# Cross-attention of a decoder layer: one transpose per head for the maxima, a reordered opening, moved value projections and border waits

## Chip, cores and metric

The kernel runs on one core of a Trainium2 chip. The metric is the device time of one execution in microseconds (us). TensorE multiplies matrices into PSUM, VectorE, ScalarE and GpSimd work on elements, SyncE issues DMAs and waits for them. Each engine runs its own instructions in order; semaphores tie them together.

## The reference

A pre-norm decoder layer with B=4, T=512, D=512: self-attention, cross-attention over 1024 context rows, and a quantised feed-forward. The part around the change, for each batch:

```python
Q = (query @ Wq).reshape(b, q_len, G, Hpg, dh) / sqrt(dh)   # G=4 groups, Hpg=4, dh=32
K = (key @ Wk).reshape(b, kv_len, G, dh)
V = (value @ Wv).reshape(b, kv_len, G, dh)
scores = einsum('bqghd,bkgd->bghqk', Q, K) + m * (k - q)    # m: slope of the head
w = softmax(where(mask, scores, min), axis=-1)
out = einsum('bghqk,bkgd->bqghd', w, V).reshape(b, q_len, 512) @ Wo
x = x + out
```

## The kernel before

Three phases follow one another, each with its own block of five instruction streams. A block ends with a barrier over all engines; behind it GpSimd clears the phase's semaphores (line 44).

**Cross-attention** (from line 780) handles 64 heads (4 batches of 16, in groups of 4). A head has four units (c, r), and the loop over `UNITS` is the same on every engine. Scores are made twice. In the first form (line 1353, tile `ps_a`, two banks) queries are rows; VectorE takes the maximum of each row (line 1224). The maxima of a head, 128x4 for each of four query tiles, with three columns of slope values beside them, are transposed (line 1365) and copied as rows 96 to 99 of `Q` (line 1233), so that the second form (line 1341, `ps_b`, keys are rows) gives scores less their maximum. ScalarE takes the exponential (line 1082) and its rounded part (line 1109), GpSimd the remainder (line 1275), and TensorE multiplies both with the values (lines 1381, 1382, 1386). First scores run two heads ahead of the second, value products three units behind.

`ORDER` (line 864) lists twelve jobs of a batch: projections of queries, keys and values and the output products of the batch before. A job has four pieces, one a unit, and a new job begins every five units. The first two value jobs lie in the eight units ahead of the first exponential. Output products wait for the normalised group `aT` (line 1301).

**Opening** (lines 1194, 1303): keys of batch 0, statistics, normalisation, transposes, queries of groups 0 and 1; then SyncE spreads keys and queries over partitions by DMA (lines 918 to 946), three DMAs a head and five a group of keys. All of group 0 must have landed before the first scores. **End** (lines 1000 to 1014): the last four output tiles are added to x1 rows from a ring of three buffers and stored; SyncE waits for all stores. The feed-forward loads x2 rows and an identity, and GpSimd computes the reciprocal deviation (line 1729).

## Time and profile before

| | |
|---|---|
| median of 3 runs | 1785.76 us (1784.31 to 1786.4) |
| profiled execution | 1786.3 us, its span 1784.2 us |
| TensorE busy | 1650.0 us (92%) |
| ScalarE / GpSimd / VectorE busy | 1236.8 / 1175.4 / 1158.1 us |
| mean granted clock of TensorE | 0.982 |
| DMA moved | 110.76 MB |

Self-attention ends at about 667 us, cross-attention at about 1456, the feed-forward at 1781. The busy times are sums over phases with different limits; the chain of work that ended last covers only the feed-forward, so the two phases before must be read from timelines.

### The profile page before, as it was taken

Reading aid. Unit: us, or ns where it says so; the run is one execution under the profiler, and the core shown is the slowest. Engines: PE = TensorE matmul, PEld = TensorE weight load, DVE = VectorE, ACT = ScalarE, POOL = GpSimd, SP = SyncE. Lnnn points to the kernel's source line nnn. Section 1 sums busy time; section 2 is a strip of 40 time slices with the busy share of each in tenths; the row PEclk is TensorE's granted clock in tenths of the full one; section 3 lists DMA queues with packets and bytes.
Section 4 is the critical chain, followed back from the end, with each engine's and each line's share of the span. In section 5 each row is a group of like instructions: output and inputs, shape, how many; then the busy total and the mean of one; then the engine's idle time right before and its main releaser. Section 6 shows DMA issues by size and latency. Waiting matters only on the chain. (4 is left out here: it accounts for less than half of the span.)

```text
span 1784.2 us, 24902 instructions
## 1 busy us (share of the span) xinstructions
PE 1650.0 (92%) x8112; PEld 1161.7 (65%) x8112; DVE 1158.1 (65%) x2031; ACT 1236.8 (69%) x2018; POOL 1175.4 (66%) x1080
## 2 busy tenths in 40 slices
...
GB/s 225 95 60 85 95 126 113 85 103 105 101 13 13 31 12 73 130 42 13 77 77 45 27 74 70 25 36 28 63 24 34 114 113 1 25 25 37 25 19 24
DMA packets 57647, 110.76 MB, mean 62 GB/s; under 512 B 9132, under 2 KB 13996, under 8 KB 57136
## 3 DMA queue, kind: packets, MB, share of 16 engines
...
## 5 line engine op out<-in xcount | busy, mean ns | idle before, releaser
L1275 POOL TENSOR_TENSOR x_p_lo<-x_p,x_p_hi 128x1024 fp32r<-128x1024 f32 x192 | 455.5, 2384 | 258.5 <-ACT x_p_hi L1109 258.0
L1224 DVE TENSOR_REDUCE x_maxes<-x_ps_a 128x1 f32<-128x1024 f32 x256 | 312.8, 1222 | 227.6 <-PE x_ps_a L1353 226.1
L1082 ACT ACTIVATE x_p<-x_ps_b,x_any_valid 128x1024 f32<-128x1024 f32 x256 | 285.1, 1114 | 129.6 <-PE x_ps_b L1341 128.2
L1341 PE MATMUL x_ps_b<-x_Q,x_K 100*128 100x512 f32 x512 | 226.4, 523 | 5.6 <-ACT x_p L1082 4.4
L1109 ACT ACTIVATE x_p_hi<-x_p 128x1024 fp32r<-128x1024 f32 x192 | 203.2, 1058 | 4.8
L1353 PE MATMUL x_ps_a<-x_K,x_Q 99*128 99x512 f32 x512 | 164.8, 403 | 10.6 <-DMA x_Q<-x_p_lo 8.8
L1381 PE MATMUL x_ps_o<-x_p_hi,x_V 128*96 128x512 f32 x384 | 157.1, 409 | 1.2 <-POOL x_p_lo L1275 1.2
L1341 PEld LDWEIGHTS x_ps_b<-x_Q,x_K 100*128 100x128 f32 x512 | 90.2, 190 | 97.8 <-issue 74.0
L1382 PE MATMUL x_ps_o<-x_p_lo,x_V 128*96 128x512 f32 x384 | 150.9, 393 | 0.0
L435 ACT ACTIVATE a_work<-a_ps_s,a_neg_max,a_q_r 128x256 f32<-128x256 f32 (+1 forms) x256 | 133.9, 539 | 4.5 <-DVE a_neg_max L535 4.5
L627 POOL TENSOR_TENSOR a_work<-a_work,a_inv_den 128x1024 f32<-128x1024 f32 (+1 forms) x64 | 109.9, 1717 | 18.7 <-DVE a_inv_den L575 18.7
L1386 PE MATMUL x_ps_o<-x_p,x_V 128*96 128x512 f32 x256 | 120.4, 591 | 0.0
L1353 PEld LDWEIGHTS x_ps_a<-x_K,x_Q 99*128 99x128 f32 x512 | 94.0, 190 | 40.4 <-issue 10.8
L616 POOL TENSOR_TENSOR a_q_r<-a_q_ss,a_half_neg 128x4 f32<-128x4 f32 x64 | 65.1, 1017 | 76.7 <-DVE a_q_ss L553 74.9
L633 PE MATMUL a_ps_out<-a_w_hi,a_aT_hi 128*128 128x512 f32 x256 | 108.8, 425 | 1.4 <-DVE a_aT_lo L496 1.4
L634 PE MATMUL a_ps_out<-a_w_lo,a_aT_hi 128*128 128x512 f32 x256 | 102.6, 401 | 0.0
L635 PE MATMUL a_ps_out<-a_w_hi,a_aT_lo 128*128 128x512 f32 x256 | 102.5, 400 | 0.0
L420 ACT ACTIVATE a_qT_hi<-a_ps_front 128x512 fp32r<-128x512 f32 x64 | 38.2, 597 | 64.8 <-PE a_ps_front L694 64.8
L602 POOL TENSOR_TENSOR a_work<-a_q 128x512 f32<-128x512 f32 x64 | 66.5, 1038 | 18.8 <-ACT a_q L458 18.8
L496 DVE TENSOR_TENSOR a_aT_lo<-a_ps_a,a_aT_hi 128x512 fp32r<-128x512 f32 x64 | 44.3, 692 | 51.0 <-ACT a_aT_hi L379 50.5
L1382 PEld LDWEIGHTS x_ps_o<-x_p_lo,x_V 128*96 128x96 f32 x384 | 62.4, 163 | 22.4
L1381 PEld LDWEIGHTS x_ps_o<-x_p_hi,x_V 128*96 128x96 f32 x384 | 62.0, 161 | 22.9 <-POOL x_p_lo L1275 2.0
...
## 6 DMA issues: line engine op xcount, KB each, us to landing
...
```

The costliest lines, as they stand in the source:

```text
L435: act.activation(p[:, c % 2, j, 0:w], ps_s[:, j, 0:w], ACT.Exp, scale=q_r[:, c % 4, j:j + 1], bias=neg_max[:, c % 2, j:j + 1], accum_out=r ...
L627: pool.tensor_tensor(out=p[:, c % 2, :, 0:w], in0=p[:, c % 2, :, 0:w], in1=inv_den[:, c % 2, :].unsqueeze(2).to_broadcast([P, G1, w]), op= ...
L633: pe.matmul(out_ap, hi, rhs_hi, start=start, stop=False)
L1082: act.activation(p[:, r, :, :], ps_b[:, :, :], ACT.Exp, scale=any_valid[:, b % 2:b % 2 + 1]).then_inc(exp_ready, 1)
L1109: act.activation(p_hi[:, r], p[:, r], ACT.Copy).then_inc(hi_ready, 1)
L1224: dve.tensor_reduce(out=maxes[:, h2, r, 3:4], in_=ps_a[:, :, :], axis=mybir.AxisListType.XY, op=ALU.max)\
L1275: pool.tensor_tensor(out=p_lo[:, r], in0=p[:, r], in1=p_hi[:, r].bitcast(F32), op=ALU.subtract).then_inc(lo_ready, 1)
L1341: last = pe.matmul(ps_b[:, j, :], K[0:ROWS + 4, g, kb * P:(kb + 1) * P], Q[0:ROWS + 4, hh, :], start=True, stop=True)
L1353: last = pe.matmul(ps_a[:, j, :], Q[0:ROWS + 3, h2, r * P:(r + 1) * P], K[0:ROWS + 3, g2, j * 512:(j + 1) * 512], start=True, stop=True)
L1381: pe.matmul(bank[0:ROWS, :], vs, p_hi[:, rw, j], start=(rw == 0 and j == 0), stop=False)
L1382: last = pe.matmul(bank[0:ROWS, :], vs, p_lo[:, rw, j], start=False, stop=False)
L1386: last = pe.matmul(bank[0:ROWS, :], V32[:, bw % 2, j, gw, :], p[:, 3, j], start=False, stop=(j == 1))
```

## The change

- The slope columns and maxima of a head stand in one 128x128 buffer, 32 columns apart, two buffers in turn; one transpose makes four blocks of rows, copied by four casts. VectorE refills the slope columns.
- The opening: barrier without a wait for the x1 stores (SyncE waits later); statistics first, slope rows split between VectorE and GpSimd, memsets on GpSimd, key rows in two parts; head 0's rows are copied by ScalarE and VectorE and not by DMA; the first eight first scores alternate between `ps_a` and `ps_b`; the output weights load later.
- One of the first two value jobs moves into the loop; in later batches the first value job comes ahead of the output products. The jobs of batch 0 shift by five units, the norms of the next batch by a head.
- The last four x1 rows are all loaded ahead; the barrier waits for one store. The feed-forward waits for the others before its loads, and the identity is loaded once for all phases.
- Semaphores are cleared in ranges.

```diff
...
-    for s in sems:
-        nc.gpsimd.sem_clear(s)
+    nums = sorted(s.num for s in sems)
+    first = 0
+    for k in range(1, len(nums) + 1):
+        if k == len(nums) or nums[k] != nums[k - 1] + 1:
+            nc.gpsimd.sem_clear(range(nums[first], nums[k - 1] + 1))
+            first = k
...
+        ident = stack.enter_context(nc.sbuf_tensor("ident", [P, P], F32))
+        ident_bf = stack.enter_context(nc.sbuf_tensor("ident_bf", [P, P], BF16))
+        rows = stack.enter_context(nc.sbuf_tensor("rows", [P, 3, D], F32))
+        x1_stored = [stack.enter_context(nc.semaphore(f"x1_stored{j}")) for j in range(2)]
+        x2_stored = [stack.enter_context(nc.semaphore(f"x2_stored{j}")) for j in range(3)]
...
-            for j in range(2):
-                sp.wait_ge(x1_stored[j], 16 * (TILES // 2))
...
+            act.activation(ident_bf[:, :], ident[:, :], ACT.Copy).then_inc(round_ready, 1)
...
-        maxes = sb("maxes", [P, HX, TPB, 4])
+        maxes = sb("maxes", [P, 2, P])
...
-        ORDER = (("Q", 2, 0), ("Q", 3, 0), ("K", 0, 1), ("K", 1, 1), ("out", 0, -1), ("out", 1, -1), ("out", 2, -1), ("out", 3, -1),
-                 ("Q", 0, 1), ("V", 0, 1), ("V", 1, 1), ("Q", 1, 1))
+        ORDER = (("Q", 2, 0), ("Q", 3, 0), ("K", 0, 1), ("K", 1, 1), ("V", 0, 1), ("out", 0, -1), ("out", 1, -1), ("out", 2, -1),
+                 ("out", 3, -1), ("Q", 0, 1), ("V", 1, 1), ("Q", 1, 1))
...
-        for b in range(-1, B):
-            jobs = [(8 * b + 4 * (n - 9), (name, i, 0)) for n, (name, i, later) in enumerate(ORDER) if name == "V"] if b < 0 else \
-                [(4 * HX * b + 5 * n, (name, i, b + later)) for n, (name, i, later) in enumerate(ORDER) if 0 <= b + later < B]
+        def add_job(u, job):
+            for k in range(4):
+                pieces[divmod(u + k, 4)] = job, k
+            finished.append(job)
+            finished_at[divmod(u + 3, 4)] = job
+        add_job(-4, ("V", 0, 0))
+        add_job(0, ("V", 1, 0))
+        for b in range(B):
+            for n, (name, i, later) in enumerate(ORDER):
+                if 0 <= b + later < B:
+                    add_job(4 * HX * b + 5 * (n + 1 if b == 0 and n < 5 else n), (name, i, b + later))
...
-            return (hh - 2, b + 1) if r == 3 and 0 <= c < HEADS and 2 <= hh < 6 and b + 1 < B else None
+            i = hh - (2 if b else 3)
+            return (i, b + 1) if r == 3 and 0 <= c < HEADS and 0 <= i < TPB and b + 1 < B else None
...
+        def scores_bank(n):
+            return ps_b if n < 8 and n % 2 else ps_a
+        def queries_spread(g, b):
+            return 192 * (b + 1) - (48 if g == 0 else 0)
+        def last_rows(i):
+            return hT[:, 0, :] if i == 0 else x1t[:, (TPB * (B - 1) + i) % 3, :]
...
-                for j in range(HPG):
+                for j in range(1 if b == g == 0 else 0, HPG):
...
             load_mask(0)
-            sp.dma_start(wo_sb[:, :, :], wo.rearrange("(c p) n -> p c n", p=P)).then_inc(wo_in, 16)
...
             spread_keys(0, 3)
+            sp.dma_start(wo_sb[:, :, :], wo.rearrange("(c p) n -> p c n", p=P)).then_inc(wo_in, 16)
+            for j in range(2):
+                sp.wait_ge(x1_stored[j], 16 * (TILES // 2))
...
-            for i in range(3):
-                load_residual(B - 1, i)
+            for i in range(TPB):
+                k = TPB * (B - 1) + i
+                if i:
+                    sp.wait_ge(x2_stored[k % 3], 16 * 4)
+                sp.dma_start(last_rows(i), x1_rows[k * P:(k + 1) * P, :]).then_inc(res_in[k % 3] if i else last_in, 16)
...
-                sp.dma_start(x2_rows[k * P:(k + 1) * P, :], x1t[:, k % 3, :]).then_inc(x2_stored[k % 3], 16)
-                if i == 0:
-                    load_residual(B - 1, 3)
-            for j in range(3):
-                sp.wait_ge(x2_stored[j], 16 * len(range(j, TILES, 3)))
+                sp.dma_start(x2_rows[k * P:(k + 1) * P, :], last_rows(i)).then_inc(x2_stored[k % 3] if i else last_stored, 16)
+            sp.wait_ge(last_stored, 16)
...
+            def first_k(i):
+                act.wait_ge(first_k_made, i + 1)
+                act.activation(k_hi[:, i * 512:(i + 1) * 512], ps_b[:, i, :], ACT.Copy).then_inc(first_k_hi_ready, 1)
+            def key_rows_of(groups):
+                act.activation(K[ROWS:ROWS + 4, groups, :], key_rows[ROWS:ROWS + 4, :].unsqueeze(1).broadcast_to(
+                    [4, groups.stop - groups.start, S]), ACT.Copy).then_inc(k_rows_ready, 1)
+            first_k(0)
+            act.wait_ge(rows_in, 32)
+            key_rows_of(slice(0, 1))
...
-            for i in range(2):
-                act.wait_ge(first_k_made, i + 1)
-                act.activation(k_hi[:, i * 512:(i + 1) * 512], ps_b[:, i, :], ACT.Copy).then_inc(first_k_hi_ready, 1)
+            first_k(1)
...
-            act.wait_ge(const_in, 48)
-            act.activation(K[ROWS:ROWS + 4, :, :], key_rows[ROWS:ROWS + 4, :].unsqueeze(1).broadcast_to([4, GX, S]), ACT.Copy)\
-                .then_inc(k_rows_ready, 1)
...
+                if i == 0:
+                    act.activation(Q[0:DH, 0, :], bank[0:DH, :], ACT.Copy, scale=QSCALE).then_inc(head0_hi_ready, 1)
+                    act.wait_ge(head0_hi_ready, 1)
+                    act.activation(Q[DH:2 * DH, 0, :], Q[0:DH, 0, :].bitcast(F32), ACT.Copy).then_inc(head0_hi_ready, 1)
+                    act.wait_ge(head0_lo_ready, 1)
...
+            key_rows_of(slice(1, GX))
+            act.wait_ge(k_rows_ready, 2)
...
-            dve.memset(half_neg[:, :], -0.5).then_inc(ones_ready, 1)
-            dve.memset(V[:, :, :, :, 2 * DH:].bitcast(F32), 1.0).then_inc(ones_ready, 1)
-            dve.memset(V32[:, :, :, :, DH:2 * DH], 0.0).then_inc(ones_ready, 1)
-            dve.memset(V32[:, :, :, :, 2 * DH:], 1.0).then_inc(ones_ready, 1)
+            dve.memset(half_neg[:, :], -0.5).then_inc(half_ready, 1)
...
+            def slope_columns(c):
+                if c >= 2:
+                    dve.wait_ge(max_made, c - 1)
+                at = maxes[:, c % 2, :].rearrange("p (j a) -> p j a", a=32)
+                dve.tensor_copy(at[:, :, 0:3], slope_cols[:, c % HX, 0:3].unsqueeze(1).broadcast_to([P, TPB, 3])).then_inc(slope_ready, 1)
...
+            for i in range(TPB):
+                statistics(0, i)
+            variances(0)
+            first_k(0)
+            biases(0)
+            mask_to_row(0)
+            first_k(1)
+            valid(0)
+            dve.wait_ge(cols_in, 16)
+            dve.wait_ge(ones_ready, 1)
+            for c in range(2):
+                slope_columns(c)
+            dve.wait_ge(rows_in, 32)
+            dve.tensor_copy(Q[ROWS:ROWS + 4, 0:HPG, :], slopes[ROWS:ROWS + 4, 0:HPG].unsqueeze(2).broadcast_to([4, HPG, T]))\
+                .then_inc(q_rows_ready, 1)
...
+                if i == 0:
+                    dve.wait_ge(first_q_made, 1)
+                    dve.wait_ge(head0_hi_ready, 1)
+                    dve.scalar_tensor_tensor(out=Q[2 * DH:3 * DH, 0, :], in0=bank[0:DH, :], scalar=QSCALE, in1=Q[0:DH, 0, :].bitcast(F32),
+                                             op0=ALU.mult, op1=ALU.subtract).then_inc(head0_lo_ready, 1)
...
-                    if n == 0:
-                        dve.wait_ge(maxes_in, 16)
-                    if c + 2 >= HX and r == 0:
-                        dve.wait_ge(max_made, c + 2 - HX + 1)
-                    dve.tensor_reduce(out=maxes[:, h2, r, 3:4], in_=ps_a[:, :, :], axis=mybir.AxisListType.XY, op=ALU.max)\
-                        .then_inc(max_ready, 1)
+                    if c >= 0 and r == 0:
+                        dve.wait_ge(max_made, c + 1)
+                    dve.tensor_reduce(out=maxes[:, c % 2, 32 * r + 3:32 * r + 4], in_=scores_bank(n)[:, :, :], axis=mybir.AxisListType.XY,
+                                      op=ALU.max).then_inc(max_ready, 1)
...
-                    dve.tensor_copy(Q[ROWS:ROWS + 4, (c + 1) % HX, :], ps_x[0:4, :]).then_inc(max_row_ready, 1)
+                    for j in range(TPB):
+                        dve.tensor_copy(Q[ROWS:ROWS + 4, (c + 1) % HX, j * P:(j + 1) * P], ps_x[32 * j:32 * j + 4, 0:P])\
+                            .then_inc(max_row_ready, 1)
+                if r == 3 and 2 <= c + 3 < HEADS:
+                    slope_columns(c + 3)
...
+            pool.memset(maxes[:, :, :], 0.0).then_inc(ones_ready, 1)
+            pool.memset(V[:, :, :, :, 2 * DH:].bitcast(F32), 1.0).then_inc(ones_ready, 1)
+            pool.wait_ge(half_ready, 1)
...
+            pool.memset(V32[:, :, :, :, DH:2 * DH], 0.0).then_inc(ones_ready, 1)
+            pool.memset(V32[:, :, :, :, 2 * DH:], 1.0).then_inc(ones_ready, 1)
+            pool.wait_ge(rstd_ready, 1)
+            pool.wait_ge(ones_ready, 4)
+            pool.wait_ge(rows_in, 32)
+            pool.tensor_copy(Q[ROWS:ROWS + 4, HPG:, :], slopes[ROWS:ROWS + 4, HPG:].unsqueeze(2).broadcast_to([4, HX - HPG, T]))\
+                .then_inc(q_rows_ready, 1)
+            pool.wait_ge(q_rows_ready, 2)
...
-            pe.wait_ge(wo_in, 16)
-            pe.wait_ge(q_rows_ready, 1)
-            pe.wait_ge(ones_ready, 4)
+            pe.wait_ge(q_rows_ready, 2)
+            pe.wait_ge(head0_hi_ready, 2)
+            pe.wait_ge(head0_lo_ready, 1)
...
                     if r == 0:
-                        pe.wait_ge(max_row_ready, c + 1)
+                        pe.wait_ge(max_row_ready, TPB * (c + 1))
...
-                        pe.wait_ge(first_k_lo_ready, 2)
+                        pe.wait_ge(max_ready, 8)
...
                     if r == 0 and h2 % HPG == 0:
-                        pe.wait_ge(q_spread[g2], 192 * (b2 + 1))
+                        if n:
+                            pe.wait_ge(q_spread[g2], queries_spread(g2, b2))
...
-                    if n:
-                        pe.wait_ge(max_ready, n)
+                    if n == 0:
+                        pe.wait_ge(first_k_lo_ready, 2)
+                    if n == 4:
+                        pe.wait_ge(q_spread[0], queries_spread(0, 0))
+                    if n >= 2:
+                        pe.wait_ge(max_ready, n if n > 8 else n - 1)
...
                     for j in range(2):
-                        last = pe.matmul(ps_a[:, j, :], Q[0:ROWS + 3, h2, r * P:(r + 1) * P], K[0:ROWS + 3, g2, j * 512:(j + 1) * 512],
+                        last = pe.matmul(scores_bank(n)[:, j, :], Q[0:ROWS + 3, h2, r * P:(r + 1) * P], K[0:ROWS + 3, g2, j * 512:(j + 1) * 512],
...
+                    pe.wait_ge(slope_ready, c + 2)
...
-                        pe.wait_ge(max_row_ready, c + 1)
+                        pe.wait_ge(max_row_ready, TPB * (c + 1))
...
-                    for j in range(TPB):
-                        last = pe.transpose(ps_x[0:4, j * P:(j + 1) * P], maxes[:, (c + 1) % HX, j, :], ident[:, :])
-                    last.then_inc(max_made, 1)
+                    pe.transpose(ps_x[:, 0:P], maxes[:, (c + 1) % 2, :], ident[:, :]).then_inc(max_made, 1)
...
-                    if rw == 0 and kw % HX == 0:
-                        pe.wait_ge(job_read, jobs_until("V", 1, bw))
+                    if w == 0:
+                        pe.wait_ge(ones_ready, 4)
+                    if rw in (0, 2) and kw % HX == 0:
...
+            for j in range(3):
+                sp.wait_ge(x2_stored[j], 16 * 5)
...
-                if c == -3:
-                    dve.wait_ge(ident_in, 16)
-                    dve.tensor_copy(ident_bf[:, :], ident[:, :]).then_inc(const_ready, 1)
...
```

## Rows read from the trace of the kernel before

**Rows 1.** Busy time by engine in one stretch: stretch, length, PE, PEld, DVE, ACT, POOL, clock.
```profile
725.26:1437.87 712.61, 701.25 (x2784) 441.61 (x2783) 480.33 (x522) 580.46 (x629) 477.58 (x210) 1.00 0.18 53
```

**Rows 2.** Timeline of VectorE, border: start, length, instruction [idle before, releaser].
```profile
665.86 0.69 DVE L523 TENSOR_TENSOR a_work<-a_ps_out,a_xt 128x512 f32<-128x512 f32 x1 [3.16 <-PE a_ps_out L635]
...
669.13 0.06 DVE L1113 MEMSET x_half_neg<- 128x4 f32 x1 [2.59 <-PEq L113]
```

**Rows 3.** Timeline of TensorE, opening of cross-attention.
```profile
669.25 8.80 PE L1307 MATMUL x_ps_b<-shared 128*128 128x512 f32 x16 [3.43 <-PEq L113]
...
691.25 3.67 PE L1321 MATMUL x_ps_j<-x_hT,shared 128*128 128x512 f32 x8 [1.37 <-ACT x_hT L1061]
...
694.76 3.60 PE L1321 MATMUL x_ps_x<-x_hT,shared 128*128 128x512 f32 x8
...
707.21 1.19 PE L1353 MATMUL x_ps_a<-x_K,x_Q 99*128 99x512 f32 x2 [8.85 <-DMA x_Q<-x_p_lo]
...
714.76 1.05 PE L1291 MATMUL x_ps_j<-shared 128*128 128x128 f32 x8
...
725.26 0.70 PE L1341 MATMUL x_ps_b<-x_Q,x_K 100*128 100x512 f32 x2
```

**Rows 4.** Timelines of VectorE and ScalarE, opening of cross-attention.
```profile
675.88 4.42 DVE L1195 CAST x_Q<-x_slopes 4x8192 fp32r<-4x8192 f32 x1 [3.98 <-DMA x_p<-in_c_key_rows]
...
685.03 0.58 DVE L1132 TENSOR_SCALAR x_ln_bias<-x_mv,x_ln_rstd 128x1 f32<-128x1 f32 x4 [1.19 <-POOL x_ln_rstd L1258]
...
710.87 1.23 DVE L1224 TENSOR_REDUCE x_maxes<-x_ps_a 128x1 f32<-128x1024 f32 x1 [1.21 <-PE x_ps_a L1353]
...
727.84 0.41 DVE L1164 TENSOR_TENSOR x_V<-x_ps_j,x_V 128x256 fp32r<-128x256 f32 x1
...
685.28 2.93 ACT L1026 ACTIVATE shared<-shared,x_ln_bias,x_ln_rstd 128x512 f32<-128x512 f32 x4 [23.31 <-DVE x_ln_bias L1132]
```

**Rows 5.** Timeline of SyncE's DMA issues: first and twelfth of group 0's queries.
```profile
697.98 0.59 SPq L944 DMA_DIRECT2D x_Q<-x_p_hi  x1
...
704.94 0.59 SPq L946 DMA_DIRECT2D x_Q<-x_p_lo  x1
```

**Rows 6.** Timeline of TensorE in the middle of the stage, around one head's transposes.
```profile
1007.65 0.60 PE L1365 MATMUL x_ps_x<-x_ident,x_maxes 128*4 128x128 f32 x4
1008.00 0.48 PE L1381 MATMUL x_ps_o<-x_p_hi,x_V 128*96 128x512 f32 x1
1008.32 0.39 PE L1382 MATMUL x_ps_o<-x_p_lo,x_V 128*96 128x512 f32 x1
```

**Rows 7.** Groups by line, 740 to 1436: busy us, mean ns, idle before, releaser.
```profile
L1275 POOL TENSOR_TENSOR x_p_lo<-x_p,x_p_hi 128x1024 fp32r<-128x1024 f32 x189 | 448.4, 2384 | 213.7 <-ACT x_p_hi L1109 213.1
...
L1233 DVE CAST x_Q<-x_ps_x 4x512 fp32r<-4x512 f32 x62 | 42.4, 684 | 3.6 <-PE x_ps_x L1365 1.7
```

**Rows 8.** Waits of TensorE, 740 to 1436: us in total, times, longest.
```profile
PE x_ps_j L1301 <- POOL x_aT L1265: 3.0, 3, 1.1
```

**Rows 9.** Timeline of VectorE, border into the feed-forward.
```profile
1450.94 0.69 DVE L1172 TENSOR_TENSOR x_x1t<-x_ps_a,x_x1t 128x512 f32<-128x512 f32 x1 [0.17 <-PE x_ps_a L1418]
...
1454.90 0.69 DVE L1172 TENSOR_TENSOR x_x1t<-x_ps_a,x_x1t 128x512 f32<-128x512 f32 x1 [3.27 <-DMA x_x1t<-x_scratch]
...
1458.06 0.06 DVE L1607 MEMSET f_half_neg<- 128x1 f32 x1 [2.47 <-PEq L785]
```

**Rows 10.** Timelines of VectorE and TensorE, opening of the feed-forward.
```profile
1463.50 0.21 DVE L1663 TENSOR_SCALAR f_ln_bias<-f_mv,f_ln_rstd 128x1 f32<-128x1 f32 x1 [4.31 <-POOL f_ln_rstd L1729]
...
1466.52 0.23 DVE L1666 CAST f_ident_bf<-f_ident 128x128 bf16<-128x128 f32 x1 [2.81 <-DMA f_ident<-in_c_ident]
...
1469.39 0.59 PE L1762 MATMUL f_ps_q<-f_ident_bf,f_hq 128*128 128x128 bf16 x4 [17.62 <-ACT f_hq L1590]
```

**Rows 11.** Line 44, windows at 1440 and 1770: count, ns, first and last start.
```profile
L44 POOLq EVENT_SEMAPHORE_RANGE_CLEAR  x64: 44/44/44, 1458.0 to 1462.7; - x64
...
L44 POOLq EVENT_SEMAPHORE_RANGE_CLEAR  x48: 44/44/44, 1780.9 to 1784.2; - x48
```

119 lines of the change are left out of this document (53 added, 66 removed).

## The prediction

> **What bounds the kernel now.** I read three views in this order: busy time by stage, then TensorE's timeline in the middle of cross-attention, then every engine's timeline at the two borders between phases and at the end. In the 712.6 us from the first exponential's scores to the last head, TensorE is busy 98% at full granted clock; no other engine passes 82% [rows 1]. So here a saved TensorE slot is saved time, as long as the next engine keeps pace. Outside this stage the picture turns over: between the last operation of self-attention (665.86 + 0.69 = 666.55) and the first probability scores at 725.26, TensorE mostly waits [rows 2, 3], and the same holds from the last output product of cross-attention to the feed-forward's first transposes [rows 9, 10]. These are chains of single operations, and each is to be followed link by link.
>
> **Border into cross-attention.** The last x1 rows are ready at 666.55, yet VectorE's next operation starts at 669.13: 2.59 us in which SyncE issues the last store, waits for its landing and joins the barrier [rows 2]. The change moves that wait far behind, onto SyncE, ahead of loads that have many microseconds to spare. The issue and the barrier stay, about 0.65 us, so the new phase opens at about 667.2: 1.9 us less. GpSimd's clears, now a few ranges, end at once, which it needs, because it gets the memsets.
>
> **The opening, link by link.** Before: VectorE waits for the constants, then spends 4.42 us on one cast of the slope rows, and only then takes the statistics; biases at 685.03, normalised rows from 685.28, query products at 691.25, queries at 698.36, and the scores of head 0 only at 707.21, 8.85 us after the products ended: SyncE issues the five DMAs of the keys and then twelve of the queries one after the other, the latter from 697.98 to 704.94, and the scores start 2.3 us after the last issue [rows 3 to 5]. After, from 667.2:
> - Keys: 8.80 us for 16 matmuls [rows 3], the first half ready at 671.8, the second at 676.2. ScalarE copies the first (0.6), writes a quarter of the key rows (1024 columns, 0.6 at the rate of VectorE's cast) and is free by 673.3 [rows 4].
> - Statistics and variance took 685.03 - 1.19 - 680.30 = 3.5 us [rows 4]; they start at once and end at 670.9. VectorE's first key remainder follows (to 673.3), then the biases. The four normalisations take 2.93 [rows 4]: 673.5 to 676.5.
> - From their end to the first query product there were 691.25 - 688.21 = 3.0 us [rows 3, 4]; the same here, with the second key copy in between, gives 679.5. Two groups of query products take 3.55 each [rows 3]: 683.1 and 686.6.
> - Head 0's 96 rows no longer travel by DMA: copies of 32x512 by ScalarE and VectorE right after the first group, done at about 684.6. The keys of group 0 need five DMAs at 0.63 apart from 677.9 and 2.3 to land: 683.4, hidden. TensorE can start the scores of head 0 at 686.6, 20.6 us earlier than before.
> - Heads 1 to 3 need nine DMAs from 686.0: 9 x 0.63 + 2.3 [rows 5] gives 693.9. The first four maxima (1.23 us each [rows 4], over two banks, no longer in step with TensorE) end by 693.1. The next four start at 693.9 + 1.2, take 4 x 1.23 and share VectorE with the four short row copies (1.0): 701.0. The first probability scores wait for all eight, since they share the second bank: about 700.9 instead of 725.26. **Opening, border included: 24.4 us.**
>
> What the trace does not show here is GpSimd's price for memsets and for the cast of 4x6144 slope values that TensorE awaits. Its nearest row takes 2.33 ns a column with two inputs [rows 7]; at that rate the 2816 memset columns and 6144 cast columns would end at 667.3 + 1.0 + 8960 x 2.33 ns = 689.2, 2.6 us late, but then the scores of heads 1 to 3 still wait for 693.9, and nearly all of it is absorbed. At half that rate it ends at 678.7, unseen. I take nothing, and up to 4 us in the range. Were VectorE's cast rate (4.42 / 8192) right, it would be earlier still. The page "GPSIMD Engine Reference", section "Engine selection", of the Trainium skill puts one-input work at roughly line rate and two-input work at about half VectorE's speed; no row here has a one-input GpSimd operation.
>
> **Value projection moved.** One of the two value jobs (four pieces) leaves the opening for the first four units of the loop and pushes the later jobs back by five units. The first units are paced by the exponential, but the displaced query job then lies where TensorE is the bound. A piece occupies up to 1.05 us [rows 3]; where the exponential paces the unit, part is hidden. Between 0 and 4.2 us I take **+2.7**. With the next batch's values ahead of the output products, those come five units (over 10 us) later than the last normalised group of the batch; TensorE now waits for it three times, 3.0 us together [rows 8]: **-3.0**.
>
> **The transposes.** Four of 128x4 become one of 128x128 for each of 64 heads. They start at 1007.65; the value products behind them at 1008.00, and the second of those 0.32 later instead of the usual 0.23 [rows 6]. So four cost 0.35 + 0.09 = 0.44 us of TensorE. One costs 0.09 and the same 0.09 behind it: 0.17, a saving of 0.27 a head. It would be 0.15 if the wider weights can't be loaded under the product before, and 0.35 at most, if the exposed load goes too. 64 x 0.27 = 17.3; the last two heads and some units paced by the exponential keep part: **-15.5** (bounds 9 and 22).
> Of this, the Trainium skill's page "TensorE: Matmul & The Clock Gate", part 4, says that a transpose takes about 275 ns in a kernel's context and that access latency dominates. Each lasts 272 ns here too, but they overlap: four are through in 0.35, so I count starts and not durations.
>
> **VectorE pays.** One cast of 4x512 (0.68 us) becomes four of 4x128, and a copy of slope columns is added per head. From PSUM 512 columns take 0.68 and 256 take 0.41 [rows 4, 7], so 128 take 0.28; four are 1.0 to 1.1, plus 0.2: 0.55 more a head, of some 11 us in which VectorE has 33% free [rows 1]. They stand ahead of the next maximum (unit 2) or behind one (unit 3), and TensorE's next scores wait for that; the maximum starts with over 1 us in hand in most units. I take **+0.4** for the units with statistics.
> A rule against the change: the Trainium skill's page "VectorE: DVE Perf Modes" has a fixed cost of about 150 cycles an instruction and advises tiles of 512 elements or more. By it (an estimate: 4 x (0.156 + 0.133) = 1.16 us) the four copies cost 0.5 us more than one; the rows above say nearly the same, and it is covered.
>
> **Border into the feed-forward.** The fourth residual waited 3.27 us for its x1 rows, which could load only after an earlier store from the same buffer; the one before it waited 0.17. Now they are loaded in time: 3.1 less. Behind it VectorE idles 2.47 for the last store to land; only issue and barrier remain, 0.6: 1.9 less [rows 9]. Then GpSimd spends 1458.0 to 1462.7 on 64 clears [rows 11], while the variance is ready at 1463.50 - 4.31 = 1459.19; the power, 0.56 long, can't have started before 1462.8, 3.6 late [rows 10]. And the maximum of h stands in VectorE's queue behind a cast that waits 2.81 us for the identity and starts at 1466.52, while h was ready at about 1464.5 (bias by 1463.7, one normalisation of 0.73 [rows 4]): 2.0 more [rows 10]. Both go. ScalarE's table load and warm-up end about 2.1 us after the opening, together with the biases, and become the next link. The x2 rows 2 to 6 now load only after all stores have landed (about 1455.4); by the code's order they are wanted only behind the first tile's quarters. **-10.5** in all, the chain behind this is the same and shifts.
>
> **The end.** The last 48 clears run from 1780.9 to 1784.2, behind everything, 0.07 us apart [rows 11], and the last of them ends the span. With about three ranges: **-3.1**. If a range costs by its length, nothing is gained here (and 3.6 fewer above).
>
> **Sum** against the profiled execution's 1786.3 us (its span of 1784.2 and 2.1 around it, taken as unchanged): -24.4 + 2.7 - 3.0 - 15.5 + 0.4 - 10.5 - 3.1 = -53.4, so 1732.9; the median lies 0.5 lower, so **1732.4**.
>
> **Rivals.** (a) GpSimd or the DMAs hold the opening: the 4x6144 cast at more than two-input cost, the constants late, or the first groups' DMAs landing later than 2.3 us. Against it stands the slack counted above; it would give back 6 to 10 us: 1740. Chance 0.12. (b) The transposes' slots don't become time: ScalarE's 580.5 us are 9.1 a head [rows 1], and heads without jobs may be paced by it, or the wide weight load is exposed. Then 4 us are left of 15.5: 1744. Chance 0.10; for it the units in which TensorE waits for the exponential, against it 98% busy. (c) The borders don't do what they say: the waits that were moved, or the range clears, come back at the same size elsewhere, 8 of 13.6 us: 1740. Chance 0.04. (d) Transposes are serial after all, by the page's duration: three times 0.272 a head are 52 instead of 17: 1697. Chance 0.02, as starts 0.09 apart speak against it. (e) **Slower than before**: VectorE's four row copies each cost as much as the wide one, 0.68. That adds 2.04 us a head between the maxima of units 2 and 3; with about 0.9 us in hand in a unit (VectorE's idle 33% over four units), TensorE's next scores come 1.1 late, 73 us in all: 1805. The other gains are worth 53.4 / 64 = 0.83 a head, so the change loses from 2.41 us for the four on (0.68 + 0.9 + 0.83), 0.60 a copy. The row of 256 columns at 0.41 speaks against it [rows 4]. Chance 0.02. The forecast keeps 0.70.
>
> **Range.** The forecast's own bounds (opening +4 and -3, transposes +6 and -6, values -2.7 and +1.5, clears) give about 1724 to 1741; with (a) to (c) taken in and (d), (e) left out, 1723 to 1745. A measurement of this kernel tells about 0.2% from no change; faster 0.97, same 0.01, slower 0.02.
>
> **What would show it.** In the profile after: VectorE's first operation of cross-attention within 0.8 us after the last of self-attention; first scores near 687 and first probability scores near 701; transposes one a head, and heads with jobs near 11.2 us instead of 11.5; no wait for the normalised group; four casts a head well under 0.35 us each; 11.4 us between the feed-forward's first operation and its first transposes shrunk to under 6; a few clears at the end. It would be wrong if TensorE shows new idle time before the maxima's scores, or if the scores of heads 1 to 3 wait past 696.

## The result

The changed kernel takes 1742.65 us (median of 4 runs, 1740.04 to 1745.32), the kernel before 1785.46 (median of 4, 1784.31 to 1786.4). The ratio is 0.9761, with a 95% interval of 0.9744 to 0.9778: 42.8 us less. The forecast was 1732.4 with a range of 1723 to 1745, so the time lies inside the range, but 10 us above the likeliest value. No term of the range was this part of the difference: it was wide for other reasons. The profiled execution took 1742.52, its span is 1740.7.

The main stage first, in the windows of the changed kernel: stretch, length, busy time of TensorE, its weight loads, VectorE, ScalarE and GpSimd, granted clock, DMA share, GB/s. It answers to [rows 1].

```profile
699.34:1407.04 707.70, 691.59 (x2624) 433.68 (x2624) 524.95 (x772) 580.32 (x630) 477.35 (x210) 0.99 0.19 57
```

TensorE has 9.7 us less to do, but the stretch is only 4.9 us shorter: 16.1 us of it are not busy, where there were 11.4. New idle time has come in, and the largest piece of it lies at one place. VectorE and TensorE in the changed kernel, start, length, instruction, and in brackets the idle time before it with what ended it:

```profile
711.88 0.69 DVE L1157 BATCH_NORM_STATS2 x_stats<-shared 128x6 f32<-128x512 f32 x1 [9.37 <-DMA shared<-x_scratch]
712.61 0.18 DVE L1159 BATCH_NORM_AGGREGATE x_mv<-x_stats 128x2 f32<-128x6 f32 x1
712.71 1.19 DVE L1286 TENSOR_REDUCE x_maxes<-x_ps_a 128x1 f32<-128x1024 f32 x1
...
713.96 1.22 PE L1435 MATMUL x_ps_a<-x_K,x_Q 99*128 99x512 f32 x2 [5.26 <-DVE x_maxes L1286]
```

VectorE's statistics of the next batch stand 9.37 us on the x1 rows. The maximum behind them in VectorE's queue is what TensorE waits for (5.26 us). SyncE's queue in the changed kernel tells why the rows are late; each line is a DMA's issue:

```profile
699.41 0.53 SPq L953 DMA_DIRECT2D x_K<-x_k_hi  x1
...
705.70 0.59 SPq L981 DMA_DIRECT2D x_wo<-in_L_xattn_Wo  x1
706.40 1.79 SPq L924 DMA_DIRECT2D shared<-x_scratch  x3
```

The four loads of x1 (L924; this view ends behind the third) are issued last, from 706.40, behind every spread of keys and queries and behind wo. The loop starts at 699.34.

**Where the time went, part by part.** I cut each profiled execution at nine instructions that all kernels have. The columns are: end of self-attention's last VectorE operation; from there to the first operation of cross-attention (border); to the first scores; to the first probability scores; to the transposes of the fourth head; to those of the 64th; to the first operation of the feed-forward; to its first transposes; to its last VectorE operation; to the end of the span; and last, all from the end of self-attention on. Every number is a difference of two starts (or ends) in the timelines; the end of the span was taken to 0.1 us, so the last two columns are good to 0.05.

```
                 self   border scores  prob   4th    64th    FFN    FFN   last   end    all behind
                 ends                         head   head   opens  transp. op           self-attn.
before          666.55  2.58   38.08  18.05  26.15  667.43  39.22  11.33  308.22  6.59   1117.65
changed         664.20  0.84   17.56  16.74  35.59  653.07  34.53   5.60  308.92  3.65   1076.50
e1              663.98  0.83   17.56  16.80  28.99  653.08  34.51   5.59  309.90  3.66   1070.92
e2              662.51  0.83   19.25  16.91  36.41  668.85  34.51   5.59  307.65  3.59   1093.59
e3              661.66  0.83   19.26  17.30  35.62  651.38  34.52   5.59  308.25  3.59   1076.34
e4              662.70  2.58   38.02  19.84  27.71  667.82  39.28  11.42  309.60  3.63   1119.90
e5              666.09  0.83   19.29  17.13  29.25  657.68  34.52   5.60  308.27  3.64   1076.21
e6              665.71  0.83   17.59  19.74  29.96  651.72  34.50   5.60  309.52  3.63   1073.09
e7              666.62  2.56   19.29  16.71  29.03  653.15  36.22   5.60  307.77  3.65   1073.98
e8              664.99  0.83   26.50  14.77  29.01  653.08  34.52   5.60  309.93  3.57   1077.81
e9              667.96  0.83   19.28  20.20  29.27  653.17  34.52   5.59  308.91  3.67   1075.44
e10             665.58  0.83   19.28  17.35  29.36  653.11  34.52   5.60  306.38  3.59   1070.02
e11             667.23  0.83   19.28  17.31  25.46  653.10  34.51   5.60  309.50  3.68   1069.27
e12             665.16  0.83   19.28  17.15  24.46  651.58  34.51   5.60  309.67  3.66   1066.74
```

Columns scatter where no edit touches them: the end of self-attention (661.66 to 667.96), the feed-forward (306.4 to 309.9), the way to the first scores, which is 17.6 or 19.3, and in the kernel before and e4, whose code is the same there, the next two (18.05 and 19.84, 26.15 and 27.71). Of the 43.5 us between the spans of before and changed, 2.35 are such scatter in self-attention. The loop column is steady: in the kernels in which nothing of the loop was edited it is 653.07 to 653.17. So an edit of 2 us is read here from its own column and not from the total. The experiments ran in three groups (e1 to e4, e5 to e8, e9 to e12); the kernel before, run in each, took 1786.1, 1785.4 and 1785.4 us, so medians of different groups compare to about 0.7 us.

In e2, e3, e5 and e9 to e12 the larger value of the "scores" column comes from one group of instructions, the first query products (e7 has another cause, see there). First the changed kernel, then e10:

```profile
676.05 3.67 PE L1398 MATMUL x_ps_j<-x_hT,shared 128*128 128x512 f32 x8 [1.85 <-ACT x_hT L1096]
```

```profile
677.46 5.37 PE L1399 MATMUL x_ps_j<-x_hT,shared 128*128 128x512 f32 x8 [1.85 <-ACT x_hT L1096]
```

The same eight matmuls behind the same idle time take 3.67 or 5.37 us. What differs is TensorE's granted clock, in these windows of the changed kernel and of e10 (columns as above, the clock is the third number from the end, in parts of 2.4 GHz):

```profile
676.00:683.00 7.00, 6.95 (x17) 3.15 (x18) 5.08 (x8) 1.81 (x3) 0.23 (x1) 1.00 0.25 57
```

```profile
677.00:683.00 6.00, 5.54 (x9) 2.41 (x10) 2.70 (x4) 0.45 (x2) 1.38 (x1) 0.72 0.68 177
```

At 0.72 a part of the stretch ran at the lower of the two levels, 1.2 GHz. The kernel before and e4 differ in the same way in the first heads. TensorE waits 1.65 us for the job bank in both; behind it the first query job of the loop runs at a granted clock of 1.00 in the one (725 to 735) and 0.83 in the other (723 to 733):

```profile
728.31 1.13 PE L1297 MATMUL x_ps_j<-x_hT,shared 128*128 128x512 f32 x2 [1.65 <-DVE x_V L1164]
```

```profile
726.19 2.08 PE L1301 MATMUL x_ps_j<-x_hT,shared 128*128 128x512 f32 x2 [1.65 <-DVE x_V L1168]
```

### The profile page after: what moved, and what is told of

It is laid out like the page before. It is cut to its first block and busy times, and to the rows that moved or that the text cites. A ratio compares the mean times of both kernels' runs of the same rounds, so it can differ in the third digit from the quotient of the medians.

```text
span 1740.7 us, 24610 instructions
## 1 busy us (share of the span) xinstructions
PE 1632.4 (94%) x7920; PEld 1147.5 (66%) x7920; DVE 1202.6 (69%) x2284; ACT 1238.6 (71%) x2022; POOL 1184.2 (68%) x1085
## 5 line engine op out<-in xcount | busy, mean ns | idle before, releaser
L1286 DVE TENSOR_REDUCE x_maxes<-x_ps_a 128x1 f32<-128x1024 f32 x252 | 306.9, 1218 | 150.8 <-PE x_ps_a L1435 145.8
L634 POOL TENSOR_TENSOR a_work<-a_work,a_inv_den 128x1024 f32<-128x1024 f32 (+1 forms) x64 | 110.0, 1719 | 18.6 <-DVE a_inv_den L582 18.6
L1435 PEld LDWEIGHTS x_ps_a<-x_K,x_Q 99*128 99x128 f32 x504 | 90.5, 191 | 48.0 <-DVE x_maxes L1286 26.9
L1296 DVE CAST x_Q<-x_ps_x 4x128 fp32r<-4x128 f32 x256 | 74.1, 289 | 9.3 <-PE x_ps_x L1447 1.3
```

The lines of the kernel that those rows point to most:

```text
L634: pool.tensor_tensor(out=p[:, c % 2, :, 0:w], in0=p[:, c % 2, :, 0:w], in1=inv_den[:, c % 2, :].unsqueeze(2).to_broadcast([P, G1, w]), op= ...
L1286: dve.tensor_reduce(out=maxes[:, c % 2, 32 * r + 3:32 * r + 4], in_=scores_bank(n)[:, :, :], axis=mybir.AxisListType.XY, op=ALU.max).then_ ...
L1435: last = pe.matmul(scores_bank(n)[:, j, :], Q[0:ROWS + 3, h2, r * P:(r + 1) * P], K[0:ROWS + 3, g2, j * 512:(j + 1) * 512], start=True, st ...
```

## The experiments

The theory: the parts act as forecast, and the difference to the forecast is one new stall, the x1 loads behind all the spreads. Its main rivals: the transposes' slots give less than counted, or the opening and the borders give less.

**e1, x1 loads early.** On SyncE, the waits and the four loads move up:

```
 spread_keys(0, 0)
+for j in range(2):
+    sp.wait_ge(x1_stored[j], 16 * (TILES // 2))
+sp.wait_ge(first_norm_made, TPB)
+for i in range(TPB):
+    load_x1(1, i)
 spread_queries(0, 0)
...
 sp.dma_start(wo_sb[:, :, :], ...)
-(the same five lines)
```

> The changed kernel with one step of SyncE moved: the waits for x1 and for the first norms, and the four loads of batch 1's x1 rows, stand right behind the spread of the first key group, ahead of all the other spreads and of wo, instead of behind them. Theory A (in the changed kernel the loop starts some 24 us earlier, but these loads only about 17 us earlier, and VectorE's statistics of batch 1, queued ahead of a maximum that TensorE waits for, stand 9.4 us on them): the wait of 9.37 us ahead of the third or fourth BATCH_NORM_STATS2 goes, and the kernel takes 1733 to 1735 us. Theory B (TensorE is behind for other reasons in the first heads, half clock or missing spreads, and only shows up under that name): at most 2 us are won, 1740.5 to 1742.6, and another idle row of 5 us or more stands on TensorE between 700 and 735. The four issues put ahead of the first Q spreads cost 2.5 us if those are what the fourth maximum of head 1 waits for: 1736 then.

Measured: 1736.87 us (1736.27 to 1737.89), ratio 0.972 (0.9693 to 0.9747), 5.8 less than the changed kernel and above theory A's 1733 to 1735. The stall is gone from the timeline, the "4th head" column falls by 6.60, and what else moves is the feed-forward's scatter (0.98). So the cause is shown, but my price was too high: I took VectorE's 9.4 us of waiting, and what counts is TensorE's, 5.26 and some slower matmuls behind it (1.22 and 1.91 us where the usual are 0.73 and 1.05). The four issues ahead of the query spreads delay nothing: the fifth quarter of scores still starts 7 us behind the first.

**e2, four transposes and one wide copy.**

```
-pe.transpose(ps_x[:, 0:P], maxes[:, (c + 1) % 2, :], ident[:, :])
+for j in range(TPB):
+    last = pe.transpose(ps_x[0:4, j * P:(j + 1) * P], maxes[:, (c + 1) % 2, 32 * j:32 * j + 4], ident[:, :])
...
-for j in range(TPB):
-    dve.tensor_copy(Q[ROWS:ROWS + 4, (c + 1) % HX, j * P:(j + 1) * P], ps_x[32 * j:32 * j + 4, 0:P])
+dve.tensor_copy(Q[ROWS:ROWS + 4, (c + 1) % HX, :], ps_x[0:4, :])
```

> The changed kernel with the maxima of a head turned by four transposes of 128x4 into one bank's four partitions, as before, and moved into Q by one cast of 4x512, as before; all else as changed (two column buffers, slope columns copied for each head). Theory A (the transposes take TensorE's time, which sets the loop, 0.33 us a head by the traces): 64 x 0.33 = 21 us more, less what the cast gives back; 1758 to 1764. Theory B (they take their time only in slots in which TensorE waits anyway, as rival (b) had it): within 3 us of 1742.6. Theory C (VectorE bounds as much as TensorE in the changed kernel; one cast is 0.56 us a head shorter than four): between, 1746 to 1755.

Measured: 1759.29 us (1758.09 to 1764.8), 16.6 more than the changed kernel; the loop column 15.78 more for 60 heads, 0.26 a head. That is theory A at its lower end, and the forecast's 0.27. The rows in e2, then in the changed kernel, around one head's transposes, answer to [rows 6]:

```profile
936.26 0.60 PE L1446 MATMUL x_ps_x<-ident,x_maxes 128*4 128x128 f32 x4
936.62 0.47 PE L1464 MATMUL x_ps_o<-x_p_hi,x_V 128*96 128x512 f32 x1
936.93 0.39 PE L1465 MATMUL x_ps_o<-x_p_lo,x_V 128*96 128x512 f32 x1
```

```profile
734.93 0.27 PE L1447 MATMUL x_ps_x<-ident,x_maxes 128*128 128x128 f32 x1
734.96 0.47 PE L1464 MATMUL x_ps_o<-x_p_hi,x_V 128*96 128x512 f32 x1
735.27 0.39 PE L1465 MATMUL x_ps_o<-x_p_lo,x_V 128*96 128x512 f32 x1
```

Four transposes are through in 0.36 us, one in 0.03, though each is shown 0.27 long. The product behind either is 0.08 late (0.31 instead of 0.23). So four cost 0.44 and one 0.11, 0.33 a head, of which 0.26 became time. The run puts back VectorE's one wide copy together with the transposes, and that the other 0.07 is the cheaper copy is not shown.

**e3, slope columns on ScalarE.** The copy `at[:, :, 0:3] <- slope_cols` leaves VectorE; ScalarE makes it in a head's last quarter.

> The changed kernel with the copy of a head's slope columns (128x12) on ScalarE in the fourth quarter of a head, instead of on VectorE. Theory A (VectorE's copy, which reads and writes SBUF alone, is held while GpSimd subtracts, 0.16 us free and up to 1.09 held, and a maximum behind it is late for TensorE in the heads without a job): the heads of 9.7 us go back to 9.1, TensorE's wait for maxima falls from 18.6 us towards the 6.3 of the kernel before, and the kernel takes 3 to 8 us less, 1735 to 1740. Theory B (TensorE is not held by it: its waits for maxima have another source): no change, 1741.5 to 1743.5. If ScalarE is what comes next (it is busy 580 of 708 us), the copy there costs as much as it gives: 1742 to 1746.

Measured: 1740.99 us (1740.05 to 1742.85), 1.7 less; the loop column 1.69 less. Theory A is right on the mechanism and wrong by a factor of two or more on the size (3 to 8 us; 1740.99 lies just above its 1740). In the heads without a job the 9.68 and 9.07 us that alternate in the changed kernel become 9.2 to 9.3: the held copies had cost something in every second head. But they do not go below that, since ScalarE is then what TensorE waits for. The last two rows show how the wait moves, first the changed kernel, then e3 (TensorE's weight loads in 760 to 1400; busy, mean ns, idle before and what ended it):

```profile
L1418 PEld LDWEIGHTS x_ps_b<-x_Q,x_K 100*128 100x128 f32 x472 | 82.3, 190 | 91.7 <-issue 67.5 <-ACT x_p L1121 23.2 <-DVE x_Q L1296 0.3
L1435 PEld LDWEIGHTS x_ps_a<-x_K,x_Q 99*128 99x128 f32 x458 | 81.3, 189 | 35.2 <-DVE x_maxes L1286 18.6 <-issue 1.4
```

```profile
L1435 PEld LDWEIGHTS x_ps_a<-x_K,x_Q 99*128 99x128 f32 x458 | 83.0, 189 | 28.4 <-DVE x_maxes L1288 9.7 <-issue 1.4
L1418 PEld LDWEIGHTS x_ps_b<-x_Q,x_K 100*128 100x128 f32 x474 | 82.1, 190 | 96.2 <-issue 63.9 <-ACT x_p L1132 31.9 <-DVE x_Q L1298 0.3
```

Waiting for maxima falls from 18.6 to 9.7 us, waiting for the exponential rises from 23.2 to 31.9.

**e4, the kernel before with range clears alone.** `nc.gpsimd.sem_clear(range(first, last + 1))` for each run of neighbouring semaphores.

> The kernel before with one part of the change alone: semaphores cleared by ranges. Forecast by the prediction's terms: about 3 us at the end of the kernel and the part of the second border that the 64 clears hold. The identity of the FFN is still loaded there and the waits for stores still stand, so of the 10.5 us of border and FFN opening at most 4 come from clears: 1778.5 to 1782.5. If clears run beside other work everywhere but at the end: 1782.5 to 1783.

Measured: 1782.44 us (1777.94 to 1786.26), ratio 0.9977 (0.9963 to 0.9991). The "end" column is 2.96 less, as forecast. The column from the feed-forward's opening to its transposes is not: 11.42 for 11.33. VectorE's queue in e4, to be read beside [rows 10], shows what took the place of the clears:

```profile
1459.81 0.21 DVE L1667 TENSOR_SCALAR f_ln_bias<-f_mv,f_ln_rstd 128x1 f32<-128x1 f32 x1 [0.74 <-POOL f_ln_rstd L1733]
1466.51 0.23 DVE L1670 CAST f_ident_bf<-f_ident 128x128 bf16<-128x128 f32 x1 [6.48 <-DMA f_ident<-in_c_ident]
```

That is the second theory, in which the clears run beside other work everywhere but at the end. The bias no longer waits 4.31 us for the power, but the identity comes from DRAM at 1466.51 all the same, and VectorE stands on it for 6.48 instead of 2.81. Of the 5.7 us in the feed-forward's opening, the range clears alone give nothing; they can count only together with the identity that stays in SBUF. What that identity gives alone was not run.

By the same run a range clear takes longer the more semaphores it covers. The 94, 64 and 48 single clears of the three phases became ranges of 0.55, 0.41 (0.09 and 0.33) and 0.33 us (0.06 and 0.26).

**e5, values behind the output products again** (on e1: the old list ORDER).

> The kernel of e1 (changed kernel, x1 loads early; 1736.9 us) with the job order of the kernel before: the first value job of the next batch stands behind the four output products and Q 0 again. Theory A (the prediction's term): the first output product waits for the normalised heads aT, about 1.0 to 1.4 us in each of three batches: 1739.5 to 1741. Theory B (another wait takes its place, or jobs of later heads shift so that nothing is lost): 1736 to 1738.

Measured: 1742.75 us (1741.21 to 1749.08), 5.9 more than e1; the loop column 4.60 more. Spacings of transposes show it at three heads, the 22nd, 38th and 54th, with +1.37, +1.40 and +1.69 us, one in each batch where the first output product stands behind the normalised group; what other heads lose and gain as a job slides by a head adds up to 0.1. Theory A, above its range of 1739.5 to 1741 and dearer than the 3.0 us that the wait itself showed in [rows 8].

**e6, both value jobs in the opening** (on e1: `add_job(-8, ...)` and `add_job(-4, ...)`, the jobs of batch 0 one place earlier).

> The kernel of e1 with the second value job of batch 0 in the opening again, as before the change, and the jobs of batch 0 one place earlier. The prediction had V moved at 2.7 us more in the loop against 3.8 us less in the opening. In e1 the opening waits for Q spreads and for VectorE's maxima, and its V pieces run at a granted clock of 0.5 to 0.7. Theory A: a piece there costs 1.3 to 1.9 us on TensorE's path and 0.7 in the loop: 2 to 5 us more, 1739 to 1742. Theory B: the pieces fill the waits of the opening (the Q spread of 2.15 us, the maxima) and the loop gains a job's time: 1733 to 1736.

Measured: 1740.69 us (1736.81 to 1741.09), 3.8 more than e1, inside theory A. By columns: 2.94 more to the first probability scores, 0.97 more to the fourth head, 1.36 less in the loop. Moving the job is worth about 2.5 us by these columns. In the loop alone it costs 1.36 - 0.97 = 0.4 us: with the job back in the opening the first heads are not shorter but longer.

**e7, the waits at both borders back** (on e1: `sp.wait_ge(x1_stored[j], ...)` at the end of self-attention, `sp.wait_ge(x2_stored[j], 16 * 5)` at the end of cross-attention).

> The kernel of e1 with the waits for stores back at both borders: the wait for x1's stores at the end of self-attention, and the wait for x2's three store semaphores at the end of cross-attention. Theory A (the prediction's terms: a store's landing of about 1.7 us stands at the first border and one of about 2 at the second): 3 to 4.5 us more, 1740 to 1741.5, VectorE's first idle row of cross-attention back from 0.8 to 2.6 us and that of the FFN from 0.9 to 2.5. Theory B (something else is late at the borders and the waits are hidden): 1736 to 1738.

Measured: 1743.96 us (1741.62 to 1746.58), 7.1 more than e1, of which the two borders are 2.56 - 0.83 = 1.73 and 36.22 - 34.51 = 1.71, a little under the forecast's 1.9 for each. Another 1.73 lies in the "scores" column, and here it is not the query products, which take 3.67 as in e1. It is the key products, which now stand behind a longer wait. First the changed kernel, then e7:

```profile
665.15 7.10 PE L1385 MATMUL x_ps_b<-shared 128*128 128x512 f32 x16 [1.68 <-PEq L123]
```

```profile
669.33 8.80 PE L1389 MATMUL x_ps_b<-shared 128*128 128x512 f32 x16 [3.44 <-PEq L123]
```

All three kernels with this wait have it: idle 3.43 to 3.46, then 8.80 us in the kernel before [rows 3] and in e7 (granted clock 0.81 over these products) and 10.09 in e4 (0.70). In the other eleven TensorE stands 1.67 to 1.71 us and the products take 7.1 at 1.00. So in e7 the first border's wait cost 1.73 + 1.70 us, twice its length. In the profiled executions, 5.7 us apart, the rest is scatter: 2.64 more in self-attention and 2.13 less in the feed-forward.

VectorE at the two borders in e7:

```profile
669.18 0.06 DVE L1156 MEMSET x_half_neg<- 128x4 f32 x1 [2.56 <-PEq L123]
...
1423.58 0.06 DVE L1693 MEMSET f_half_neg<- 128x1 f32 x1 [2.56 <-PEq L794]
```

These are the first operations of both phases. In the changed kernel they read:

```profile
665.04 0.06 DVE L1152 MEMSET x_half_neg<- 128x4 f32 x1
...
1420.97 0.69 DVE L1216 TENSOR_TENSOR rows<-x_ps_a,rows 128x512 f32<-128x512 f32 x1 [0.17 <-PE x_ps_a L1501]
1422.53 0.06 DVE L1689 MEMSET f_half_neg<- 128x1 f32 x1 [0.87 <-PEq L792]
```

The fourth residual (1420.97) waits 0.17 us where it waited 3.27 [rows 9].

**e8, head 0's queries by DMA** (on e1: `for j in range(HPG)` in the spread, without the three operations of ScalarE and VectorE that write head 0's rows).

> The kernel of e1 with head 0's queries spread by DMA like the others, instead of written by ScalarE and VectorE, so that the first scores wait for the spread. In e1 the fifth quarter of scores starts at 689.5 on that spread, 7 us after VectorE's subtraction, and the first at 682.4. Theory A: the first scores go to about 688.5 and the fifth to 693, and all behind it 3.5 to 4.5 us later: 1740.5 to 1741.5. Theory B (the opening is bound by VectorE's maxima and the V pieces, which can go ahead of the scores): under 1.5 us, 1736.5 to 1738.5.

Measured: 1744.53 us (1741.84 to 1745.67), 7.7 more than e1; first scores 8.94 later, 2.03 of it given back before the probability scores. Both theories had it too small. I had reckoned with the 7 us that the spread of the second head takes in e1, but with head 0 in it there are twelve issues in the row, not nine, and all four heads land on one semaphore:

```profile
683.27 0.55 SPq L970 DMA_DIRECT2D x_Q<-x_p_hi  x1
...
690.21 0.59 SPq L972 DMA_DIRECT2D x_Q<-x_p_lo  x1
```

```profile
692.32 1.19 PE L1423 MATMUL x_ps_a<-x_K,x_Q 99*128 99x512 f32 x2 [8.38 <-DMA x_Q<-x_p_lo]
```

That is nearly the wait of 8.85 in the kernel before [rows 3]. These three small operations are the largest piece of the opening's gain that a run took back. Query products of both take 3.67, so the clock has no part in the 8.94.

**e9, one bank for the first scores** (on e1: `scores_bank` gives ps_a always, each quarter waits for the maximum before it).

> The kernel of e1 with the first eight quarters of scores in one bank, as before the change: each waits for VectorE's maximum of the one before. In e1 they alternate between two banks, with maxima 1.14 us apart, up to the fifth, which waits for head 1's Q spread (idle 2.15 us). Theory A: the first four go from 1.14 us apart to about 2.1, which the spread hides for the most part, and the last four, between V pieces, to 2.05 each: first scores to first probability scores 18 to 19.5 us for 16.8, the kernel 1738 to 1739.5. Theory B (the Q spread and the V pieces set this stretch and the second bank is worth nothing): 16.5 to 17.3 us, 1736.5 to 1737.5.

Measured: 1742.35 us (1740.55 to 1745.21), 5.5 more than e1; the "prob" column 3.40 more (20.20 for 16.80; 2.9 more than in e10 to e12, whose query products ran at the slower rate as e9's did), and 1.72 are those query products. Theory A, above its range of 18 to 19.5 and of 1738 to 1739.5: the maxima go to between 2.0 and 2.6 us apart, and the spread hides none of it, since the fifth scores start 10.0 us behind the first instead of 7.1.

**e10, GpSimd's cast later** (on e1: `pool.wait_ge(mask_ready, 2)` ahead of the cast of 4x6144).

> The kernel of e1 with GpSimd's cast of the slope rows (4x6144, 5.46 us) waiting until VectorE's mask rows are made. In e1 the two mask rows, a TENSOR_SCALAR of 1x512 each, take 5.86 us in all and end with that cast; in the kernel before they took 0.85. Theory A (VectorE's operation from SBUF to SBUF is held for as long as GpSimd's cast runs): 0.85 us again, the second K subtraction up to 5 us earlier, and what VectorE has from SBUF to SBUF behind it (any_valid, slope copies, its own cast of 4x2048) may be held in its place. Theory B (the row waits for something else, its mask's DMA or the first K): still above 4 us. On the kernel's time both say under 1 us, since the first Q products come later than either: 1736 to 1738.

Measured: 1735.71 us (1733.93 and 1737.48). The time doesn't tell it from e1; the timeline tells the theories apart. First the changed kernel, GpSimd's cast and VectorE's mask rows:

```profile
670.77 5.46 POOL L1342 CAST x_Q<-x_slopes 4x6144 fp32r<-4x6144 f32 x1
```

```profile
670.65 5.86 DVE L1177 TENSOR_SCALAR x_mask_row<-x_mask_u 1x512 f32<-1x512 uint8 x2
```

Then e10, where the cast starts behind the mask rows:

```profile
672.06 0.85 DVE L1177 TENSOR_SCALAR x_mask_row<-x_mask_u 1x512 f32<-1x512 uint8 x2
...
676.09 1.21 DVE L1182 TENSOR_REDUCE x_any_valid<-x_mask_u 128x1 f32<-128x1024 uint8 x1
677.21 1.26 DVE L1223 COPY x_maxes<-x_slope_cols 128x12 f32<-128x12 f32 x2
```

```profile
673.08 5.30 POOL L1343 CAST x_Q<-x_slopes 4x6144 fp32r<-4x6144 f32 x1 [1.07 <-DVE x_mask_row L1177]
```

The mask rows are back at 0.85, and now the slope copies are held: 1.26 for the two, which take 0.23 in the changed kernel. The first of them lasts from 677.21 to 678.41, the cast's end is 678.38. Theory A. The reduction that runs beside the cast in e10 isn't held: 1.21, as in the changed kernel, where nothing runs beside it.

**e11, values read first** (on e1: at the first quarter of head 0, `evacuate(*done)` stands ahead of ScalarE's exponential and of VectorE's maximum).

> The kernel of e1 with one change of order at the first quarter of head 0: ScalarE and VectorE take the first value job out of its bank before their exponential and maximum, not behind them. In e1 TensorE stands 2.07 us on that bank at 702.4 and works at half clock behind it. Theory A (the second value job was moved into the loop onto a bank whose reader is queued behind later work, and that is a part of what the first heads lost): first probability scores to the fourth head's transpose 26.5 to 28 us for 29.0, the kernel 1734 to 1736. Theory B (TensorE waits for VectorE's maxima in those quarters anyway): within 0.5 us of 1736.9.

Measured: 1735.79 us (1729.73 to 1738.3), ratio 0.9704 (0.9677 to 0.9731). The runs scatter more than the edit is worth, but its column doesn't: 25.46 for 28.99, 3.53 less, more than the 1 to 2.5 of theory A, whose time for the kernel it meets. TensorE's second value job in e1, then in e11:

```profile
702.41 2.08 PE L1367 MATMUL x_ps_j<-shared 128*128 128x128 f32 x8 [2.07 <-DVE x_V L1200]
704.14 1.20 PE L1418 MATMUL x_ps_b<-x_Q,x_K 100*128 100x512 f32 x2
```

```profile
705.65 1.05 PE L1373 MATMUL x_ps_j<-shared 128*128 128x128 f32 x8
706.56 0.73 PE L1424 MATMUL x_ps_b<-x_Q,x_K 100*128 100x512 f32 x2
```

Not only the wait of 2.07 goes, but also the doubled duration of what comes behind it (2.08 for 1.05, 1.20 for 0.73). The windows behind the wait in e1 and in e11 (columns as above) show the granted clock at 0.52, nearly all of it the lower level, and at 1.00:

```profile
704.00:708.00 4.00, 4.00 (x17) 3.51 (x16) 1.77 (x2) 2.17 (x2) 1.35 (x2) 0.52 0.54 126
```

```profile
705.00:709.00 4.00, 4.00 (x27) 3.38 (x25) 3.29 (x5) 3.55 (x4) 1.26 (x1) 1.00 0.57 129
```

**e12, all together** (e1 with e3, e10 and e11).

> The kernel of e1 with the slope copies on ScalarE (e3), GpSimd's cast later (e10) and the values read first (e11). If the parts add: e3 took 1.7 us off the loop by its trace (0.2 from self-attention's end to the kernel's), e11 1 to 2, e10 0: 1733 to 1735.5. If ScalarE, which the slope copies and the early read load further, comes to bind: 1736 to 1738.

Measured: 1732.94 us (1730.98 to 1736.75), ratio 0.9702 to the kernel before (0.968 to 0.9723): 9.7 less than the changed kernel and at the lower edge of the 1733 to 1735.5 expected if the parts add. Behind self-attention it takes 1066.74 us, 4.2 less than e1 although its query products ran at the slower rate. It beats both kernels.

## Why the prediction was right, and where it was not

By the order of its steps, forecast against columns:

- **Border into cross-attention**, forecast 1.9 less: 1.74 less. e7 gives 1.73 back, and 1.70 more in the key products, which I had kept at 8.80 us. The wait itself was priced rightly. The sentence that it moves ahead of "loads that have many microseconds to spare" **is the step that failed**. In the kernel before, these loads were issued at 723.93, just ahead of the loop at 725.26. The change moved the loop to 699.34, 25.9 us forward, and left the loads where I had not looked. On SyncE they stand behind 42 issues (44 in the kernel before), 29.1 us from the first of them to the loads in both, and these issues began only 17.5 us earlier. By e1 this cost 6.60 us, over half of what was missing.
- **The opening**, with the border 24.4 less forecast: 58.71 - 35.14 = 23.57 less. First scores came 17.56 us behind the first operation (19.4 forecast), heads 1 to 3 at 689.56, 24.5 behind it (26.7 forecast); this lead was lost again. The last four maxima start 2.0 to 2.6 us apart and not 1.23, since V pieces stand between the scores on TensorE, the first two of them 1.91 and 1.57 us long for the usual 1.05. The granted clock there, in windows of the changed kernel:

```profile
688.00:692.00 4.00, 2.44 (x9) 2.25 (x10) 2.23 (x2) 0.00 (x0) 0.00 (x0) 0.50 0.58 136
692.00:696.00 4.00, 4.00 (x23) 3.61 (x22) 1.84 (x3) 0.00 (x0) 0.00 (x0) 0.70 0.33 83
```

  I had left the V pieces out of this sum. So its total came out within 1 us partly because two errors cancelled, and with the clock's scatter (18.05 or 19.84 before) it is known to some 2 us only. By pieces the 23.57 are 1.74 at the border, 11.10 up to the first query products (22.12 behind the first operation before, 11.02 now), 9.41 from there to the first scores and 1.32 from there to the probability scores. e8 takes back 6.9 us by head 0's rows, e9 2.9 to 3.4 by the second bank, e6 2.9 by the value job. The 11.10, where statistics first, the split slope rows and the moved memsets act together, no run took apart. GpSimd's price, which I left between bounds, was 0.89 ns a column for the cast (5.46 us for 6144; VectorE's cast had 0.54), and 1.38 us for the memset of 1536 columns, which took VectorE 1.34. The cast held VectorE by 5 us in the slack that I had counted, so rival (a) did not occur.
- **Value projection moved**, forecast +2.7 in the loop. The first heads of e1 take 28.99 - 26.15 = 2.84 more than before, which looks like the forecast but is luck: with both jobs in the opening again (e6) they take 29.96, and by e6 the move costs the loop 0.4 us. What makes the first heads longer is above all the clock: e4, with the code of the kernel before in this stretch, takes 27.71, and e11, in which TensorE doesn't stand on the job bank and runs at 1.00 behind it, 25.46. The 3.5 of e11 are the hand-over of the one job bank, whose reader stands behind an exponential and a maximum.
- **The wait for the normalised group**, forecast -3.0: gone, and putting it back costs 4.6 (e5). I had taken the wait's own length, without what a late output product pushes.
- **The transposes**, forecast -15.5: e2 shows 15.8 in the loop and 16.6 in the medians, VectorE's four copies for one included. Rival (b), slots that don't become time, falls, and so does (d), transposes in series.
- **VectorE pays**, forecast +0.4: four copies last 1.25 us (289 ns each, 1.0 to 1.1 forecast), so rival (e) falls. The slope copy was taken as 0.2; it is 0.37 on the mean and up to 1.09, and moving it to ScalarE gave 1.7 (e3).

```profile
L1223 DVE COPY x_maxes<-x_slope_cols 128x12 f32<-128x12 f32 x61 | 22.4, 367 | 0.0
```

- **The loop as a whole** is 14.4 shorter. The parts measured one at a time would make -15.8 - 4.6 + 1.7 + 1.4 = -17.3. The 2.9 between them are open. Each part was undone alone, and where two waits end close together (the exponential and the maximum in heads without a job) undoing one shows more than it adds; that is an argument and no measurement.
- **Border into the feed-forward and its opening**, forecast -5.0 and -5.6: -4.69 and -5.73. The sum was right. Its reasoning was half right: I gave 3.6 us to the clears and 2.0 to the identity, one behind the other. By e4 they stood side by side, and taking away the clears alone gives nothing there. The 3.1 us of the fourth residual rest on its row alone (0.17 us of waiting); no run put it back. Rival (c) did not occur.
- **The end**, forecast -3.1: -2.94, and -2.96 in e4. Seven clears are left in the whole kernel:

```profile
L47 POOLq EVENT_SEMAPHORE_RANGE_CLEAR  x7: 45/88/529, 664.9 to 1740.4; - x7
```

A range costs from 0.045 to 0.53 us. By e4's ranges length does count, but 64 semaphores cost 0.41 us and not the 4.7 of 64 single clears [rows 11].

So most mechanisms held, and the largest two terms (opening, transposes) came out within 1 us each. Behind self-attention the profiled executions are 41.15 us apart where 53.4 were forecast. Of the missing 12.25 us, 6.6 are one queue that was not followed, 3.7 are in the loop, 0.8 in the opening and 0.7 in the feed-forward, which no edit touches; the 2.35 us by which self-attention happened to end earlier gave a part back. The prediction's own list had the sign to look for: it would be wrong "if TensorE shows new idle time before the maxima's scores", which is the row at 713.96.
